# An adaLN feed-forward block on one core: f, x and the weights arrive with d on the partitions

## The reference

```
bias = embed[stage[b]]                       # one value for each row s
q    = x[b] + bias[:, None]
p    = softmax(q @ f[b].T)                   # [s, t]
y    = (p @ f[b]) @ H                        # H: Hadamard matrix, 256 x 256
yq   = round_and_clip(y / scale) * scale     # scale: largest |y| of a row / 7
out  = x[b] + yq @ ternary(weight).T         # ternary: -1, 0, 1 times the mean |w| of an output row
```

## Time and profile before

| | |
|---|---|
| median of 3 runs | 104.66 us (104.31 to 106.77) |
| profiled execution: span from its first to its last instruction | 102.9 us |
| what lies around the span, from the median | 1.8 us |
| TensorE busy | 94% of the span |
| VectorE busy | 85% |
| ScalarE busy | 74% |
| GpSimd busy | 47% |
| HBM read, written | 8.72 MB, 4.19 MB |

### The profile page before, as it was taken

How to read it: one execution, slowest core, us unless ns; L and a number is a source line. 1 busy time by engine, 2 the same in 40 slices (tenths; PEclk the granted TensorE clock), 3 DMA queues, 4 the chain that set the end, 5 groups by cost and what they waited for, 6 DMA issues and landing times.

```text
span 102.9 us, 2603 instructions
## 1 busy us (share of the span) xinstructions
PE 96.4 (94%) x801; PEld 91.0 (88%) x801; DVE 87.0 (85%) x221; ACT 76.2 (74%) x196; POOL 48.5 (47%) x72
## 2 busy tenths in 40 slices
PE   5999999999999999999999999999999999999640
PEld 2579899999999999999999999999999999899420
DVE  1067898899989898999989998989899998988881
ACT  3354878878796978787878889697978784786820
POOL 5144499804443435354545454343435454505880
PEclk9999999999999999999999999999999999999995
DMA  2896721326269464838282735546472121221126
GB/s 68 294 275 162 274 83 68 135 51 204 51 210 157 171 188 113 244 31 289 52 300 51 273 84 204 153 155 202 114 242 79 44 63 71 51 102 48 54 102 204
DMA packets 14718, 14.70 MB, mean 143 GB/s; under 512 B 7922, under 2 KB 8824, under 8 KB 14712
## 3 DMA queue, kind: packets, MB, share of 16 engines
q1 hardware_dynamic: 14400, 14.36, 46.8%
q10 hardware_dynamic: 312, 0.27, 0.8%
HBM read 8.72 MB, written 4.19 MB: 126 GB/s over the span
## 4 chain that ended last, share of the span: by engine, by line
PE 86%; DVE 6%; ACT 3%; issue 1%; DVEq 0%
PE score_bank L477 21%; PE xh_bank L477 19%; PE fh_bank L477 14%; PE prob_bank L466 7%; PE q_bank L466 6%; PE f_bank L466 6%; PE out_bank L535 6%; PE out_bank L443 3%; ACT prob L697 2%; DVE xh_bank L1016 1%; DVE last_result L1022 1%; DVE abs_max L996 1%; PE q_bank L477 1%; PE f_bank L477 1%; DVE abs_max L984 1%
## 5 line engine op out<-in xcount | busy, mean ns | idle before, releaser
L356 POOL TENSOR_TENSOR result<-scaled,x_all 128x512 f32<-128x512 f32 x13 | 16.6, 1280 | 21.4 <-DVE scaled L854 20.8
L348 POOL TENSOR_TENSOR code<-code,magic 128x512 bf16<-128x512 f32 x13 | 13.6, 1043 | 12.1 <-ACT code L675 12.1
L691 ACT CAST fh_hi<-fh_bank 128x512 fp32r<-128x512 f32 x16 | 9.4, 589 | 8.6 <-PE fh_bank L477 8.6
L697 ACT ACTIVATE prob<-score_bank,neg_max 128x256 f32<-128x256 f32 x30 | 14.0, 478 | 1.1 <-DVE neg_max L897 1.1
L477 PE MATMUL fh_bank<-had,f_hi 128*128 128x256 f32 x64 | 14.0, 300 | 0.0
L868 DVE TENSOR_TENSOR prob_lo<-prob_bank,prob_hi 128x512 fp32r<-128x512 f32 x16 | 11.0, 690 | 3.3 <-ACT prob_hi L687 3.3
L477 PE MATMUL score_bank<-f_hi,q_hi 128*128 128x256 f32 x60 | 13.2, 302 | 0.0
L675 ACT ACTIVATE code<-xh_bank,inv_scale 128x256 f32<-128x256 f32 x30 | 12.7, 481 | 0.3 <-DVE inv_scale L851 0.2
L477 PE MATMUL fh_bank<-had,f_lo 128*128 128x256 f32 x64 | 12.8, 282 | 0.0
L666 ACT CAST f_hi<-f_bank 128x512 fp32r<-128x512 f32 x15 | 8.8, 588 | 4.5 <-PE f_bank L466 4.4
L477 PE MATMUL xh_bank<-fh_hi,prob_hi 128*128 128x256 f32 x60 | 12.1, 283 | 0.0
(11 more groups left out here) (148 smaller groups left out, 236.0 us busy)
## 6 DMA issues: line engine op xcount, KB each, us to landing
f_nat<-f_dram SPq DMA_DIRECT2D x16, 256.0 KB, 2.8
x_all<-x_dram SPq DMA_DIRECT2D x16, 256.0 KB, 3.0
out_dram<-result SPq DMA_DIRECT2D x14, 256.0 KB, 2.0
w_raw<-weight_dram SPq DMA_DIRECT2D x1, 256.0 KB, 5.0
out_dram<-result SPq DMA_DIRECT2D x2, 128.0 KB, 1.8
out_dram<-last_result ACTq DMA_DIRECT2D x2, 128.0 KB, 1.8
code_t<-code SPq DMA_TRANSPOSE x13, 2.5
had_block<-hadamard_dram SPq DMA_DIRECT2D x1, 64.0 KB, 3.1
```

What stands on the lines that cost most here:

```text
L348: nc.gpsimd.tensor_tensor(as_rows(code16[:, b.k]), as_rows(code), magic[:, :].broadcast_to([P, W]), ALU.subtract).then_inc(code16_ready, 1)
L356: nc.gpsimd.tensor_tensor(result[:, b.k], as_rows(scaled[:, b.k]), x_all[:, b.at], ALU.add).then_inc(result_ready, 1)
L691: nc.scalar.copy(fh_hi[:, b.k], fh_bank[:, :, :]).then_inc(fh_hi_ready, 1)
L697: a = nc.scalar.activation(prob[:, t], score_bank[:, t], ACT.Exp, bias=neg_max[:, b.k, t:t + 1], accum_out=row_sum[:, b.k, t:t + 1])
```

## The change

The host hands over f and x a second time in another layout, with d on the partitions (`f_turned`, `x_turned`), and the weight turned as well. x in its own layout is still loaded, for the residual, but only in step i-3 (`x_all`, just ahead of the DMA transpose on SP). Nothing of f or q is turned on TensorE. With rows on the free axis the bias is a row that is the same in all partitions: one product per batch of 12 rows (embed in high and low parts) with 128 columns that pick the stage's rows (`row_picks`, spread by GpSimd) puts it in a bank, and VectorE adds it to `xt` (`add_bias`). The low part of f moves from VectorE to GpSimd (`split_f`). The high parts of f and q are copied by ScalarE out of SBUF, those of f one step earlier. The orders of stages are new. The weight is compared against rows of bounds spread by a product with ones.

```diff
 # SP
-                    wait(sp, f_in_bank, b.at - 1)
-                    sp.dma_start(f_nat[:, b.k], f_dram[b.at]).then_inc(f_loaded[b.k], 16)
+                    wait(sp, f_lo_ready, b.at - 2)
+                    sp.dma_start(as_row(ft[:, b.k]), ft_dram[b.at]).then_inc(ft_loaded[b.k], 16)
                     wait(sp, q_ready, b.at - 1)
+                    sp.dma_start(as_row(xt[:, b.k]), xt_dram[b.at]).then_inc(xt_loaded[b.k], 16)
+                if (b := batch(LAG_QUANT)) and b.at < B - 2:
                     sp.dma_start(x_all[:, b.at], x_dram[b.at]).then_inc(x_loaded[b.k], 16)
 # POOL
+            def split_f(b):
+                wait(pool, f_hi_ready, b.at + 1)
+                nc.gpsimd.tensor_tensor(f_lo[:, b.k], ft[:, b.k], f_hi[:, b.k].bitcast(F32),
+                                        ALU.subtract).then_inc(f_lo_ready, 1)
+            def pick_rows(b):
+                wait(pool, bias_in_bank, b.at - 1)
+                nc.gpsimd.tensor_copy(row_picks[:, b.k], one_hot[:, b.at].broadcast_to([2 * STAGES, P])
+                                      ).then_inc(picks_ready, 1)
 # in step: pick_rows(i+2), split_f(i), out_scales(i-3), code16(i-3), result(i-4)
 # weight_signs, after w_bounds_ready:
+                for over, bound in ((w_over_below, w_below), (w_over_above, w_above)):
+                    nc.gpsimd.tensor_tensor(over[:, :, :], w_t[:, :, :],
+                                            bound[:, :].unsqueeze(1).broadcast_to([P, C, O]),
+                                            ALU.subtract).then_inc(w_over_ready, 1)
+                pool.wait_ge(w_over_ready, 1)
+                nc.gpsimd.tensor_scalar(w_neg[:, :, :], w_over_below[:, :, :], 0.0, None, ALU.is_lt
+                                        ).then_inc(w_neg_ready, 1)
+            pool.wait_ge(one_hot_ready, 1)
+            pick_rows(Batch(0, 2))
+            pick_rows(Batch(0, 3))
+            split_f(Batch(0, 1))
+            split_f(Batch(0, 2))
+            pick_rows(Batch(0, 4))
+            weight_signs()
+            for i in range(3, 2 * LOOP_FROM):
+                step(peeled(i))
 # PE
+            def biases(b):
+                wait(pe, picks_ready, b.at + 1)
+                wait(pe, q_ready, b.at - 1)
+                pe.matmul(bias_banks[b.k][:, 0], row_picks[:, b.k],
+                          embed_parts[:, :], start=True, stop=True).then_inc(bias_in_bank, 1)
             STAGES_IN_ORDER = (
-                (turn_f, LAG_LOAD_TURN), (turn_q, LAG_LOAD_TURN), (turn_prob, LAG_MIX),
-                (score, LAG_SCORE), (times_ternary, LAG_OUT), (times_hadamard, LAG_SCORE),
-                (mix, LAG_MIX))
+                (turn_prob, LAG_MIX), (score, LAG_SCORE), (biases, LAG_NEXT),
+                (times_ternary, LAG_OUT), (times_hadamard, LAG_SCORE), (mix, LAG_MIX))
 # ACT
             STAGES_IN_ORDER = (
-                (split_f, LAG_LOAD_TURN), (split_q, LAG_LOAD_TURN), (quantize, LAG_QUANT),
-                (split_prob, LAG_MIX), (add_bias, LAG_LOAD_TURN - 1), (split_fh, LAG_SCORE),
-                (exponentials, LAG_SCORE))
+                (split_prob, LAG_MIX), (quantize, LAG_QUANT), (split_q, LAG_PARTS),
+                (exponentials, LAG_SCORE), (split_fh, LAG_SCORE), (split_f, LAG_NEXT))
 # DVE
+            def add_bias(b):
+                wait(dve, xt_loaded[b.k], 16 * b.half + 16)
+                wait(dve, bias_in_bank, b.at + 1)
+                nc.vector.tensor_tensor(q[:, b.k], xt[:, b.k],
+                                        bias_banks[b.k][:, 0].unsqueeze(1).broadcast_to([P, C, S]), ALU.add
+                                        ).then_inc(q_ready, 1)
             def split_q(b):
                 wait(dve, q_hi_ready, b.at + 1)
-                low_part(q_lo[:, b.k], q_bank, q_hi[:, b.k]).then_inc(q_lo_ready, 1)
+                low_part(q_lo[:, b.k], q[:, b.k], q_hi[:, b.k]).then_inc(q_lo_ready, 1)
             STAGES_IN_ORDER = (
-                (scales, LAG_QUANT), (split_f, LAG_LOAD_TURN), (split_q, LAG_LOAD_TURN),
-                (split_prob, LAG_MIX), (sums, LAG_MIX), (maximum, LAG_SCORE),
-                (scale_out, LAG_OUT), (split_fh, LAG_SCORE))
+                (scales, LAG_QUANT), (add_bias, LAG_PARTS), (split_prob, LAG_MIX), (sums, LAG_MIX),
+                (maximum, LAG_SCORE), (scale_out, LAG_OUT), (split_q, LAG_PARTS),
+                (split_fh, LAG_SCORE))
 # head: after maximum(b1), three small operations that make the rows of bounds; after step 3:
+            dve.wait_ge(w_over_ready, 2)
+            dve.wait_ge(w_neg_ready, 1)
+            nc.vector.scalar_tensor_tensor(
+                out=tern_t[:, :, :], in0=w_over_above[:, :, :], scalar=0.0, in1=w_neg[:, :, :],
+                op0=ALU.is_gt, op1=ALU.subtract).then_inc(tern_t_ready, 1)
```

More of the change, by code:

```diff
@@ L122, in adaln_ffn_kernel @@
         last_result = sb("last_result", [P, W], F32)
-        f_bank = bank("f_bank", [P, C, S], F32)
-        q_bank = bank("q_bank", [P, C, S], F32)
+        bias_banks = [bank(f"bias_bank{k}", [P, T, S], F32) for k in range(2)]
         score_bank = bank("score_bank", [P, T, S], F32)
@@ L353, in step @@
                     wait(pool, scaled_ready, b.at + 1)
+                    wait(pool, x_loaded[b.k], 16 * b.half + 16)
                     wait(pool, stored[b.k], 16 * b.half)
@@ L604, in _ @@
             pe.wait_ge(tern_t_ready, 1)
-            pe.wait_ge(row_ready, 1)
             for i in range(4, 2 * LOOP_FROM):
                 step(peeled(i))
-            with pe.Fori(LOOP_FROM, B // 2) as half:
+            with pe.Fori(LOOP_FROM, B // 2 - 1) as half:
                 for odd in range(2):
                     step(looped(half, odd))
+            for i in range(B - 2, B):
+                step(peeled(i))
             fourth_last, third_last, second_last, last = (Batch(0, B - n) for n in (4, 3, 2, 1))
@@ L664, in split_f @@
                 wait(act, fh_in_bank, b.at - 1)
-                wait(act, f_in_bank, b.at + 1)
-                nc.scalar.copy(f_hi[:, b.k], f_bank[:, :, :]).then_inc(f_hi_ready, 1)
+                wait(act, ft_loaded[b.k], 16 * b.half + 16)
+                nc.scalar.copy(f_hi[:, b.k], ft[:, b.k]).then_inc(f_hi_ready, 1)
             def split_q(b):
-                wait(act, q_in_bank, b.at + 1)
-                nc.scalar.copy(q_hi[:, b.k], q_bank[:, :, :]).then_inc(q_hi_ready, 1)
+                wait(act, q_ready, b.at + 1)
+                nc.scalar.copy(q_hi[:, b.k], q[:, b.k]).then_inc(q_hi_ready, 1)
             def quantize_tile(to, xh, t, b):
@@ L920, in _ @@
-            b0, b1, b2 = (Batch(0, n) for n in range(3))
+            b0, b1, b2, b3 = (Batch(0, n) for n in range(4))
             dve.wait_ge(first_f_hi_ready, 1)
-            low_half(f_lo, first_f_banks, f_hi, 0)
+            low_half(f_lo, ft[:, 0], f_hi, 0)
+            dve.wait_ge(f_hi_ready, 1)
+            low_half(f_lo, ft[:, 0], f_hi, 1).then_inc(first_f_lo_ready, 1)
             dve.wait_ge(bias_in_bank, 1)
-            nc.vector.tensor_copy(bias[:, :, :].rearrange("p b t -> p t b"),
-                                  score_bank[:, :, 0:B]).then_inc(bias_ready, 1)
@@ L1013, in _ @@
             dve.wait_ge(last_out_scale_ready, 1)
+            dve.wait_ge(last_x_loaded[last.k], 16)
             for t in range(T):
```

374 lines of the change are left out of this document (160 added, 214 removed).

## The result

The changed kernel takes 115.64 us (median of 4 runs, 115.06 to 116.91). Beside it, in the same session, the kernel before took 105.72 (4 runs, 104.31 to 106.79). The ratio is 1.104 with a 95% interval of 1.097 to 1.111: slower. Some executions of each kernel are about 2% longer than its fastest for no reason in the kernel, and ratios leave these out while medians take them in, so a ratio is not always the quotient of two medians. The profiled execution took 115.06 us with a span of 113.2, so 1.86 us lie around the span. The forecast was 113.9 us, made against an execution with a span of 102.9.

A forecast was written before the change was run, and what follows sets the result against it. It took TensorE (94% busy) to bound the kernel before, with VectorE close. Span 102.9 + 3.0 (head) + 6.7 (eleven held steps) - 0.5 (tail) = 112.1, plus 1.8 around it: 113.9 us, range 102.5 to 116.5.

The forecast's parts named there:

- The bias product: TensorE, each step: one added product of 12 rows and 256 columns, put at 0.11 us, between 0 and 0.11.
- TensorE alone: TensorE's own work in a step, without eight transposes and with the bias product: 4.79 us instead of 5.56.
- The loop without the hold: Loop through neg_max, exponentials, fh_hi and fh_lo on VectorE and ScalarE if least_scale isn't held: 5.42 us a step.
- The wait of fh_lo for fh_hi: VectorE, each step: fh_lo waits for ScalarE's fh_hi copy, about 0.3 us.
- VectorE alone: VectorE's own work in a step, free of waits: 5.15 us.
- rival D: Loop: ScalarE does fh_hi in time and VectorE binds at 5.15 us a step; 98.5 us in all, chance 0.10.
- The hold: Loop: VectorE's least_scale is held until GpSimd's code16 ends; step 6.17 us, 0.61 more, 6.7 us over 11 steps.
- The loads: Loop: x loaded twice, 256 KB more a step, put at cost 0, up to 0.3 us a step if transfers queue.
- The head: Start up to scales of batch 2: at 30.3 instead of 27.35, +3.0 us, between +0.8 and +5.
- The tail: End of the kernel: starts with TensorE ahead, -0.5 us, between 0 and -1.
- B: Loop: least_scale not held, or code16 pushed behind it; loop 5.42 us, 105.7 us in all, chance 0.20.
- C: Loop and head: least_scale not held and the head doesn't stall; 101.5 us in all, chance 0.10.

The follow-up runs named there:

- e1: Changed kernel with least_scale made by two one-column operations instead of one on two columns: 108.91 us, ratio 1.028 to the kernel before.
- e7: Changed kernel with one-column least_scale and fh_lo moved on VectorE behind the next step's scales: 107.73 us, ratio 1.027 to the kernel before.
- e12: Changed kernel with only each step's DMA transpose put ahead of its loads on the queue: 113.19 us.
- e3: Changed kernel with one-column least_scale and ScalarE copying fh_hi ahead of the exponentials: 108.82 us, ratio 1.028 to the kernel before.
- e5: Changed kernel with one-column least_scale, fh_hi copied ahead of the exponentials, and the weight-bound rows made earlier on VectorE, ahead of split_fh(1): 107.57 us.
- e9: Changed kernel with one-column least_scale, late fh_lo, transposes first, nine warm-up products, GpSimd's code16(0) ahead of w_neg, tern_t reading a PSUM copy: 101.91 us, ratio 0.974.
- e8: Changed kernel with nine instead of seven warm-up products on TensorE: 115.4 us.

## Where the prediction was right, and which term of it failed

**TensorE.** The turns went and the step didn't get shorter, as forecast. The bias product was put at 0.11 us as the top of a range from 0. It costs 0.40: from the last score products to the ternary one it is 0.64 us with it (62.13 to 62.77 above) and 0.24 in the kernel before (63.01 to 63.25 in its timeline). TensorE alone therefore needs about 5.1 us a step, not 4.79; in the change this cost nothing, since TensorE waits for prob up to 0.8 us in nine of the steps. It was to be busy under 80% and was busy 83%.

**The loops.** The loop without the hold was put at 5.42; with one-column scales it is 5.51. The wait of fh_lo for fh_hi, put at 0.3 us a step, is 0.18 in the loop's steps (61.85 above). VectorE alone was put at 5.15; the version with both limits removed runs at 5.21. The forecast's rival D was out of reach for the change as it stands, since it needed three edits that the change doesn't have.

**The hold.** Forecast: least_scale comes 0.16 us after code16's start and is held to its end, mean near 0.9, loop 6.17. Measured: 0.20 us after (65.12 against 64.92), 0.86 long in this step, loop 6.17, +6.7 us in all. The mean over all fourteen is 0.787, with two in the head that were not held (0.14 and 0.15) and one that took 1.35. Held in these runs were least_scale on two columns, w_below (0.99 instead of 0.29), q_lo and tern_t with two SBUF inputs (up to 1.44 and 3.25 instead of 0.68). The GpSimd operations in whose run they ended up waiting have two inputs, with one open point: row_picks, with one input, ran for 0.28 us in the midst of tern_t's wait in e1 and gave it no opening.

The rule of the prediction (the Trainium skill, page SBUF — State Buffer, section "SBUF: two separate sides") is an exclusive lock that VectorE operations in a two-port mode take, and those with two SBUF inputs against a GpSimd operation that reads SBUF. The trace agrees for least_scale, w_below and tern_t. It doesn't for q_lo beside w_neg, which reads SBUF through its one input and ran from 20.13 to 21.65 in the changed kernel: q_lo at 20.80 kept its 0.68 us. The measurement decides.

Why two columns are held and one is not, the runs don't show by themselves. The Trainium skill, page VectorE: DVE Perf Modes, section "What auto-detection actually checks", offers a reason: the two-port mode is taken when a single source and the destination are in SBUF and their outermost dimensions of more than one element are both even, or equal. One column has no such dimension. The lengths agree (787 ns on average on two columns, 138 ns on one); no run here shows the mode itself.

**The loads.** Put at 0, and 0 they cost in the changed kernel's loop. But the reason (plenty of time) was too easy: the transposes' median from issue to landing rose from 2.5 to 3.5 us, and to 3.8 in e7, where it holds the step at 5.44.

**The head.** This is the term that failed: +3.0 us forecast, +4.2 measured. The step in it that failed is the start. The forecast left neg_max of batch 1 at 14.50 (1 us either way), and from it had GpSimd begin on the weight at 16.3; they came at 15.95 and 17.64, 1.3 us late. What stands in its place is TensorE's lower level in the opening, to which I had given neither a term nor a chance: with the opening at the upper level, in e12, neg_max comes at 14.32. The next term was too long, GpSimd's chain from there to the end of code16 of batch 0: 7.1 us (17.64 to 24.78) instead of 7.8. The transpose was too short: it landed at 28.5, 3.7 us after code16's end and not 3.2. From there to abs_max of batch 2 it took 3.0 us as forecast, and so it started at 31.58 instead of 30.3.

Up to 1.64 us of the head are the lower level's; without it the head would have been about +2.6, and the sum 112.1 - 0.4 plus 1.8, or 113.5 us, an estimate. That the chain was put too long by 0.7 us hid part of the late start, so that the span came within 1.1 us of the forecast (113.2 against 112.1) is in part luck. In the profiled executions the lower level comes and goes, in the opening and behind long waits. The Trainium skill, page TensorE: Matmul & The Clock Gate, section "Part 1: The HAM clock gate", says this of one kernel's first products: how many of them ran at the lower level differed from run to run. The openings of e12 and of the changed kernel agree. The forecast was added to an execution of the kernel before whose opening had none of it. That the median (115.64) stands another 0.6 us above the profiled execution (115.06) may have the same reason; it isn't shown, as the other executions have no trace.

**The tail.** -0.5 forecast, -0.6 measured. No run tests the reason that the forecast gave for it.

**Rivals.** B asked for code16 to start behind least_scale; it started ahead in each step from step 4 on. C and D asked for no hold at all.

## What to carry to other kernels

When work is moved off the bound, redraw the loops between the engines and also the overlaps between VectorE and GpSimd: a 0.15 us operation on the critical path, which had come 1.02 us after code16's start and now came 0.20 after it, cost 0.66 us a step, and without that the whole change is worth 0.05 (5.56 to 5.51). Compare each instruction's length with its own elsewhere in the trace, for a hold counts as busy time. When two limits lie within 0.1 us, remove both before concluding that one of them was none: fh_lo moved alone and the transposes moved alone gave 0.07 and 0.00 us a step, and both together 0.3. Before a difference between two profiled executions is put down to an edit, look whether TensorE opened at the same level in both: here this alone is worth 1.6 us.

## What the runs showed of the hardware that I had not expected

- A held operation of VectorE doesn't always get in at the next change of GpSimd operations. tern_t took 3.25 us through five of them in e1, but 1.15 in e3 and 1.93 in e7, where it got in behind the first f_lo; q_lo got in between two subtractions in e5 (1.44 us). Two columns of least_scale once took 1.35 us through three. The same multiplication on one column was never held in 28 (mean 138 ns), and neither was the reciprocal on two columns inside code16's run (0.15 us).
- The hold goes both ways: result 1.28 to 1.54 us (mean) with q_lo in its way, out_scale 0.19 to 0.67 with tern_t. An operation with one input, which didn't hold q_lo, was itself held by it: w_neg took 1.94 us instead of 1.52 when q_lo had got in just ahead of it (e9).
- A single product of 12 rows and 256 columns, put between two groups, costs 0.40 us, where products with 128 rows follow each other at 0.12 us (0.24 for two). How much of it is the change from one group to the next isn't shown.
- Two paces of TensorE for the same instructions: 0.213 and 0.118 us for 256 columns in the opening, with a granted clock of 1.00 in the views of both. Neither a wait of 0.25 nor one of 1.2 us ahead of them decides it: behind the first the pace was the lower (e8), behind the second the upper (e12).
